# The fold of the attention stage's logit pairs: from TensorE transposes to VectorE block exchanges and a round trip through memory

## What is computed

```python
x = x + 0.5 * ffn(layernorm(x))          # first feed-forward
x = x + attn(layernorm(x))               # attention over the head dimension, per token
x = x + 0.5 * ffn(layernorm(x))          # third stage: the same feed-forward again

def ffn(input):
    dots = softmax(x @ centroids.T / 0.1)            # 64 clusters
    hits = dots > 0.01
    query_sel = any(hits, axis=1); cluster_sel = any(hits, axis=0)
    row_sel = cluster_sel[assignments]
    return where(query_sel[:, None] & row_sel[None, :], x @ weight.T + bias, 0)
```

## Time and profile before

| | |
|---|---|
| median of 3 runs | 1199.72 us (1198.96 to 1200.38) |
| the profiled execution's own time | 1198.41 us |
| its span in the profile | 1196.6 us |
| TensorE busy | 1186.3 us (99%) |
| VectorE busy | 800.2 us (67%) |
| ScalarE busy | 495.5 us (41%) |
| GpSimd busy | 442.3 us (37%) |

### The profile page before, as it was taken

One profiled execution on the slowest core, in us unless ns is written; L12 is line 12 of the kernel. 1 busy time (PEld: TensorE's weight loads), 2 busy tenths in 40 slices (PEclk: granted clock), 3 DMA queues, 4 the chain that ended last, 5 costly groups with the idle time before them and its releaser, 6 DMA issues.

```text
span 1196.6 us, 24925 instructions
## 1 busy us (share of the span) xinstructions
PE 1186.3 (99%) x10072; PEld 1002.5 (84%) x10072; DVE 800.2 (67%) x1272; ACT 495.5 (41%) x718; POOL 442.3 (37%) x582
## 2 busy tenths in 40 slices
PE   7999999999999999999999999999999999999998
PEld 6888888888888888888888888888888888888887
DVE  6644654465454577787777877778777774299788
ACT  5322233222221355665656556566565654212110
POOL 1344445443425553433434334343343201050332
PEclk9999999999999999999999999999999999999999
DMA  7577767776664466565665555665556465017885
GB/s 276 155 203 240 209 199 188 237 206 178 160 188 147 111 163 174 144 170 139 162 168 143 168 142 159 169 145 166 153 149 169 120 173 190 5 71 254 299 284 199
DMA packets 344977, 208.72 MB, mean 174 GB/s; under 512 B 289440, under 2 KB 308640, under 8 KB 344864
## 3 DMA queue, kind: packets, MB, share of 16 engines
q1 hardware_dynamic: 329696, 187.73, 55.9%
q10 hardware_dynamic: 15168, 19.40, 4.7%
HBM read 118.49 MB, written 88.60 MB: 173 GB/s over the span
## 4 chain that ended last, share of the span: by engine, by line
PE 99%; DMA 0%; DVE 0%; ACT 0%; issue 0%; SPq 0%
PE ps_q L285 10%; PE ps_q L287 10%; PE ps_q L286 10%; PE ps_b L285 9%; PE ps_a L285 9%; PE ps_b L287 9%; PE ps_b L286 9%; PE ps_a L287 9%; PE ps_a L286 8%; PE ps_t L292 6%; PE ps_q L1433 3%; PE ps_q L299 3%; PE ps_q L301 2%; PE ps_q L1479 2%; PE ps_q L306 1%; DMA w_raw<-in_L_ffn_weight 0%
## 5 line engine op out<-in xcount | busy, mean ns | idle before, releaser
L318 POOL TENSOR_TENSOR var_eps<-moments,eps 128x1 f32<-128x1 f32 x96 | 18.2, 190 | 410.6 <-DVE moments L314 410.6
L285 PE MATMUL ps_a<-w_hi,odd_hi 128*128 128x512 f32 x368 | 148.1, 403 | 0.0
L287 PE MATMUL ps_a<-w_hi,odd_lo 128*128 128x512 f32 x368 | 143.8, 391 | 0.0
L286 PE MATMUL ps_a<-w_lo,odd_hi 128*128 128x512 f32 x368 | 143.4, 390 | 0.0
L635 POOL TENSOR_SCALAR f_out<-f_out,token_on 128x1024 f32<-128x1024 f32 x30 | 85.6, 2852 | 77.3 <-DVE f_out L1009 77.0
L686 POOL TENSOR_TENSOR x_ring<-x_ring,f_tmp 128x1024 f32<-128x1024 f32 x32 | 77.1, 2408 | 89.9 <-DVE best L1154 48.3
L285 PE MATMUL ps_b<-proj_hi,y_hi 128*128 128x512 f32 x256 | 103.1, 403 | 0.0
L287 PE MATMUL ps_b<-proj_hi,y_lo 128*128 128x512 f32 x256 | 100.1, 391 | 0.0
L286 PE MATMUL ps_b<-proj_lo,y_hi 128*128 128x512 f32 x256 | 99.9, 390 | 0.0
L327 ACT ACTIVATE y_tok<-x_ring,norms 128x1024 f32<-128x1024 f32 x64 | 79.7, 1245 | 42.6 <-POOL norms L323 27.5
L737 POOL TENSOR_TENSOR late<-late,mask 128x1024 f32<-128x1024 f32 x18 | 45.5, 2538 | 135.2 <-DMA late<-x_scratch 89.4
(11 more groups left out here) (219 smaller groups left out, 3110.8 us busy)
## 6 DMA issues: line engine op xcount, KB each, us to landing
xa<-in_L_attn_x SPq DMA_DIRECT2D x32, 512.0 KB, 5.1
f_tmp<-f_scratch SPq DMA_DIRECT2D x32, 512.0 KB, 4.6
x_ring<-in_L_attn_x SPq DMA_DIRECT2D x32, 512.0 KB, 3.6
f_scratch<-f_out SPq DMA_DIRECT2D x30, 512.0 KB, 4.0
x_scratch<-x_ring SPq DMA_DIRECT2D x30, 512.0 KB, 3.4
y_scratch<-xa SPq DMA_DIRECT2D x28, 512.0 KB, 3.7
ya_tok<-y_scratch SPq DMA_DIRECT2D x112, 128.0 KB, 3.3
late<-x_scratch SPq DMA_DIRECT2D x22, 512.0 KB, 7.0
```

Source lines behind the costliest of these rows:

```text
L285: pe.matmul(acc, hi[:, k, :], w_h[:, k, cols], start=(k == 0), stop=False)
L286: pe.matmul(acc, hi[:, k, :], w_l[:, k, cols], start=False, stop=False)
L287: last = pe.matmul(acc, lo[:, k, :], w_h[:, k, cols], start=False, stop=(k == KB - 1))
```

## The change

In turns 7 to 34 the pairs 16 to 30 no longer pass `fold_pair`. `copy_pair` writes its 256 columns in another order; VectorE exchanges the 32 x 32 blocks of `pair_sums` in place (`pair_turn`, in even turns, right behind line 1116); SP stores `pair_sums` to a scratch in memory (`store_pair`, behind `load_x` of the even turn) and loads it back in four DMAs of 32 partitions each, so that a partition holds one token of each tile (`load_pair`, between the load of q_head and the store of v of the same even turn). `pair_soft_in` becomes three VectorE instructions instead of four (one addition in place of copy and addition) and moves to the next, odd turn, behind line 1116 there; it waits for the four loads. `pair_soft_exp` moves from even to odd turns, `pair_soft_out` from odd to even turns. TensorE waits for `pair_copied` before `pair_logits` where it waited for `soft_in`. Pair 31 is folded as before.

```diff
+        def by_memory(u):
+            return NP <= u < 2 * NP - 1
         def pair_soft_in(dve, u):
+            if by_memory(u):
+                parts = pair_sums[:, :].rearrange("p (s h t c) -> p s t h c", s=2, h=2, c=D)
+                dve.wait_ge(pair_in, 64 * (u - NP + 1) + 16)
+                wait(dve, soft_exp, u)
+                dve.tensor_tensor(pair_exp_in[:, :].rearrange("p (t h c) -> p t h c", h=2, c=D), parts[:, 0], parts[:, 1],
+                                  ALU.add).then_inc(soft_step, 2)
...
+        def pair_turn(dve, u):
+            dve.wait_ge(pair_copied, u + 1)
+            dve.transpose(pair_sums[:, :], pair_sums[:, :]).then_inc(pair_turned, 1)
...
+                def store_pair(u):
+                    sp.wait_ge(pair_turned, u - NP + 2)
+                    sp.dma_start(pair_d, pair_sums[:, :]).then_inc(pair_stored, 16)
+
+                def load_pair(u):
+                    sp.wait_ge(pair_stored, 16 * (u - NP + 2))
+                    for b in range(T4):
+                        sp.dma_start(pair_sums[D * b:D * b + D, :].rearrange("p (h x) -> p h x", h=T4),
+                                     pair_d.rearrange("(h q) (b x) -> b q h x", q=D, b=T4)[b]).then_inc(pair_in, 16)
...
@@ SP
+                    if i >= 6 and i % 2 == 0:
+                        store_pair(NP + (i - 6) // 2)
+                    if i > NT and i % 2 == 0:
+                        load_pair(NP + (i - 6) // 2)
...
                         sp.dma_start(q_head[:, :],
                                      qkv_d[t, 0:HKV].rearrange(BY_TOKEN_GROUP, c=T4, j=2)).then_inc(q_in, 16)
+                        if i >= 6 and i % 2 == 0:
+                            load_pair(NP + (i - 6) // 2)
...
@@ ScalarE
+                    if by_memory(u):
+                        act.wait_ge(soft_in, u)
+                        act.copy(pair_sums[:, :].rearrange("p (b t c) -> p t b c", t=2, c=D),
+                                 pair_ps.rearrange("p (t b c) -> p t b c", t=2, c=D)).then_inc(pair_copied, 1)
...
-                    if i >= 6 and i % 2 == 0:
-                        pair_soft_exp(act, NP + (i - 6) // 2)
+                    if i >= 7 and i % 2 == 1:
+                        pair_soft_exp(act, NP + (i - 7) // 2)
@@ VectorE
                     if i >= 6 and i % 2 == 0:
-                        pair_soft_in(dve, NP + (i - 6) // 2)
+                        pair_turn(dve, NP + (i - 6) // 2)
+                    if i >= 7 and i % 2 == 1:
+                        pair_soft_in(dve, NP + (i - 7) // 2)
...
-                    if i >= 7 and i % 2 == 1:
-                        pair_soft_out(dve, 1, NP + (i - 7) // 2)
+                    if i >= 8 and i % 2 == 0:
+                        pair_soft_out(dve, 1, NP + (i - 8) // 2)
@@ TensorE
-                        pe.wait_ge(soft_in, NP + max(0, (i - 4) // 2))
+                        pe.wait_ge(soft_in, NP)
...
-                        pe.wait_ge(soft_in, u)
+                        pe.wait_ge(soft_in, NP)
+                        pe.wait_ge(pair_copied, u)
                         pair_logits(pe, odd_hi, odd_lo).then_inc(pair_done, 1)
...
-                    if 0 <= i - 4 < NT - 2 and i % 2 == 1:
-                        fold_pair(NP + (i - 4) // 2)
```

More of the change, by code:

```diff
@@ L47, in macaron_kernel @@
     o_d = nc.dram_tensor("o_scratch", (NT, HKV, P, D), F32, kind="Internal").ap()
+    pair_d = nc.dram_tensor("pair_scratch", (P, 2 * P), F32, kind="Internal").ap()
     STREAMED = list(range(0, NT - 2, 2))
@@ L190, in logit_at @@
         def logit_at(u):
-            return ps_q[:, 0, 0:QUARTER] if NP <= u < 2 * NP - 1 else ps_q[:, 3, QUARTER:HALF]
+            return ps_q[:, 3, QUARTER:HALF]
+        def by_memory(u):
+            return NP <= u < 2 * NP - 1
         def half(h):
@@ L240, in macaron_kernel @@
         late_in = w_in[0:6]
+        pair_stored, pair_in, pair_turned = w_in[6], w_in[7], cen_hi
         y_last_stored = cen_in
@@ L332, in pair_soft_in @@
         def pair_soft_in(dve, u):
-            parts = logit_at(u).rearrange("p (t s c) -> p s t c", s=2, c=NCL)
             logits = pair_exp_in[:, :].rearrange(BY_TILE, c=NCL)
[L336 to L340, removed]
+            if by_memory(u):
[4 more added lines that the diff above has]
+                                  ALU.add).then_inc(soft_step, 2)
+            else:
+                parts = logit_at(u).rearrange("p (t s c) -> p s t c", s=2, c=NCL)
+                dve.wait_ge(folded, u + 1 - (NP - 1 if u > NP else 0))
+                wait(dve, soft_exp, u)
+                dve.tensor_copy(logits, parts[:, 0]).then_inc(soft_step, 1)
+                dve.wait_ge(soft_step, 7 * u + 1)
+                dve.tensor_tensor(logits, logits, parts[:, 1], ALU.add).then_inc(soft_step, 1)
             dve.wait_ge(soft_step, 7 * u + 2)
@@ L764, in copy_pair @@
                     act.wait_ge(pair_done, u + 1)
-                    act.copy(pair_sums[:, :], pair_ps).then_inc(pair_copied, 1)
+                    if by_memory(u):
+                        act.wait_ge(soft_in, u)
+                        act.copy(pair_sums[:, :].rearrange("p (b t c) -> p t b c", t=2, c=D),
+                                 pair_ps.rearrange("p (t b c) -> p t b c", t=2, c=D)).then_inc(pair_copied, 1)
+                    else:
+                        wait(act, soft_in, u if u > NP else 0)
+                        act.copy(pair_sums[:, :], pair_ps).then_inc(pair_copied, 1)
                 def move_kv(k):
@@ L941, in _ @@
                 keep_third(3)
+                pair_soft_exp(act, 2 * NP - 2)
                 high_third(LAST)
@@ L1172, in _ @@
                                           ALU.add).then_inc(v_read, 1)
+                pair_soft_in(dve, 2 * NP - 2)
                 low_third(LAST)
@@ L1489, in _ @@
                 pe.wait_ge(scores_read, NT)
-                pe.wait_ge(soft_in, 2 * NP - 1)
+                pe.wait_ge(pair_copied, 2 * NP - 1)
                 pair_logits(pe, odd_hi, odd_lo).then_inc(pair_done, 1)
```

## The result

The changed kernel takes **1249.86 us** (median of 4 runs, 1245.97 to 1252.55) against 1199.39 us before (1198.96 to 1200.38): 50.5 us slower, a ratio of 1.0415 with an interval of 1.0391 to 1.0439. Slower was forecast, but +25.6 us of it; the measured loss is twice that and lies outside the range.

The account below looks back on a forecast made before the run. TensorE, busy 99% of the span, was taken as the bound. Stalls of 28.0 + 0.7 us less 2.4 us of folds made +26.3 us, 1224.7 on the profiled execution; stated forecast 1225.0 us, range 1204 to 1243.

Parts of the forecast that it names:

- What bounds the kernel, and what is removed: TensorE, busy 99% of the span, sets the time; 15 folds leave its queue at 0.16 us each.
- the 2.4 us of the folds: On TensorE, 15 folds removed at 0.16 us of starts each: 2.4 us saved.
- VectorE's shifts in odd and even turns: VectorE's work changes by +0.53 us in even turns and -0.31 us in odd ones; even-turn qk_read starts 0.39 later.
- When the wait ends: VectorE before pair_soft_in: last load issued at 714.24, landed at 716.64, VectorE free at 713.82; it waits 2.8 us.
- The fixed cost of 2.0 us: Skill's figure for any DMA; as the loads' landing time it gives a 2.4 us wait, the whole 5 us less.
- Who is queued behind it: VectorE's in-order queue hands the delay to low_third; TensorE stalls 2.15 us before pair_logits in 13 odd turns, 28.0 us.
- Turn 33: A kept half product replaces the v projection, slack is 1.75 us instead of 0.28; the stall costs 0.7 us.
- Nothing gives it back: TensorE has no idle time to absorb its stalls; the next even turn starts later from its own heads.
- the sum: Whole kernel: stalls 28.0 + 0.7 less 2.4 us of folds, +26.3 us.
- The range: Whole kernel: 1204 to 1243 us; the high end, 1244, has loads landing at 717.93 and a stall of 3.44 us.
- The rival of the backed-up queue: SP's four pair loads are held 1.05 us each behind k_head and q_head; stall 4.4 us, +58, 1257; chance 0.08.
- The rival of early loads: Pair loads land by 714.5 or so, VectorE's wait stays under 0.65 us, TensorE never stalls; 1197.3 us; chance 0.12.

Follow-up runs that it names:

- the versions without the wait: Changed kernel with pair loads earlier on SP (1197.89 us), pair_soft_in behind VectorE's statistics and the exponential at ScalarE's turn end (1197.90), or both (1196.68).
- two reductions: Kernel before, with two unused 1024-column VectorE reductions added behind line 1116 of odd turns 7 to 31: 1224.42 us, ratio 1.0211.
- three reductions: Kernel before, with three unused 1024-column VectorE reductions added behind line 1116 of odd turns 7 to 31: 1254.21 us, ratio 1.0460.

## Why the prediction went wrong, point by point

- **What bounds the kernel, and what is removed**: right. The starts of the changed kernel's even turns show the 2.4 us of the folds; the times of the versions without the wait give 1.4 to 1.5 us, with 2.4 inside their intervals. A small misreading: 12, not 13, of the 15 odd turns last 19.54 us within 0.02; turn 23 is 0.03 over, turn 11 0.13, and turn 33 has another product and lasts 22.12.
- **VectorE's shifts in odd and even turns**: right. In even turns `qk_read` starts 13.57 us behind the heads; 13.16 would be TensorE's pace, and 0.39 us of delay was forecast. But the sum takes the fold's 0.16 us off the time at which VectorE is free (713.82) and not off SP's chain (712.44), though both run behind the same heads. By its own parts the wait should read 2.66 us and the stall 2.0.
- **When the wait ends**: nearly. The first load was forecast 0.83 us behind the heads and goes out at 0.79 in turn 19. The four issues take 2.04 us there and 2.0 to 3.1 by turn, 2.5 on average (2.4 forecast). The landing of the last was put at 2.4 us and takes 2.9 in turn 19 and 1.8 to 3.3, 2.45 on average; where the issues are quick the landing is mostly slow, and in 10 of the 14 turns the last load lands 5.1 to 5.5 us behind the heads either way. VectorE's wait is 3.04 us in turn 19 and 45.1 / 14 = 3.2 on average, 2.8 forecast; it is longest, 3.3 to 4.3, in turns 7, 11, 21 and 25, where q_head's own issue takes 1.3 to 1.5 us, and in turn 13. The fixed cost of 2.0 us that the prediction took from the Trainium skill is given in the section named there for DMAs that GpSimd issues; these go out from SP and land 1.7 to 3.3 us behind their issue, median 2.3.
- **Who is queued behind it**: right, and the step that mattered. TensorE stalls 33.5 / 13 = 2.6 us a turn by the starts, 2.15 forecast. Turn 33 was put at 0.7 us and cost nothing: it counted only TensorE's slack, but VectorE too had room in that turn of the kernel before, 1.05 us before the scores, 1.54 before line 1147 and 1.34 before line 1111, and after a wait of 2.80 us its low part starts only 0.46 us later than it did. Stalls in all: 33.5 us against 28.7.
- **"Nothing gives it back"** is where it failed: the sum priced a stall at its own length. TensorE may come out of a stall at half its clock. The granted clock was full in all slices of before, and I took that for a property of the kernel; but TensorE waits for no other engine there between 400 and 1050 us, so the row said nothing of a kernel in which it idles 13 times. The missing term measured 16.4 us by the starts. With it the prediction's own sum would read 26.3 + 16.4 = +42.7 us, and with the stalls at 33.5 instead of 28.7, +47.5 in the span. The median lies 3.9 us above the profiled execution; those stand in runs without a trace and stay open.
- **The range**: its high end, 1244, came from later loads at full clock. The rival of the backed-up queue, 1257, came nearer to the time and mostly for the wrong reason: single issues of the pair's loads did reach 1.5 us, but the four took at most 3.1 us, not 4.2, and the stalls were 2.1 to 3.5 us, not 4.4; the rest of the loss is the clock.
- **The rival of early loads** (1197.3) didn't come, but the experiments that make the loads early gave its time: 1197.9, 1197.9 and 1196.7.

The Trainium skill (TensorE: Matmul & The Clock Gate, HAM oscillation) describes a kernel in which TensorE waits for a DMA in every round and begins each next piece of work at 1.2 GHz. The trace agrees in kind: granted clock 0.50 behind the stalls, though behind 10 of the 13 and not all.

## What to carry to other kernels

A queue that is busy two thirds of the time can have a third of a microsecond to spare at the one place where it counts: read slack as a distance between two starts in the same turn, not from the busy share. A DMA's result should be asked for a landing and all its issues later than it is sent; look for a stretch in which the issuing queue waits anyway. And where a change makes a TensorE that hardly idled wait, price the stall twice: once as time, once for what runs at half clock behind it.

## What the hardware showed that was not expected

TensorE's granted clock falls to 1.2 GHz behind stalls as short as 2.1 us (turn 27 of the changed kernel) and 1.9 us (one of 13 with two reductions), and behind none of the 0.8 us. Length alone doesn't decide: in the changed kernel it held after stalls of 2.6 and 2.7 us (turns 25 and 13) and fell after 2.1; with three reductions all 13 stalls were 3.0 us and it fell 9 times. Where it fell, 1.4 to 2.5 us were lost in the changed kernel, mostly 1.6. What decides in which turns it falls isn't shown.

The times scatter too: the changed kernel's runs spread over 6.6 us, those of before, in the same comparison, over 1.4. The clock explains only part of that, since the run of 1252.55 us had a mean granted clock of 0.984 and that of 1245.97 us one of 0.985; whether the rest is longer waits isn't known, as the slower runs left no trace.
